# First weights issued beside x, later loads held back, and the first two chunks' roundings reordered in a four-layer kernel

## The reference, cut to what matters

```python
def _gemma_mlp(x, gate_w, up_w, down_w):          # 256 -> 1024 -> 256
    g = x @ gate_w; u = x @ up_w
    return (gelu(g) * u) @ down_w

# layer 0: softmax over 8 experts, the two best, their shares; plus one shared MLP
x = x + sum(w_e * _gemma_mlp(x, skill_e) for the two experts) + _gemma_mlp(x, shared)
# layer 1: the expert of the largest logit: silu(x @ W_up.T + b_up) * (x @ W_gate.T + b_gate), then @ W_down.T + b_down
# layer 2: x @ (sum_g y_g * weight_g * mask).T + bias
# layer 3: x @ W_base.T + b_base + 2 * sum_e w_e * (x @ A_e.T) @ B_e.T
```

## Time and profile before

| | us |
|---|---|
| median of three executions | 504.8 |
| span of the profiled execution, first to last instruction | 503.2 |
| PE busy in it | 495.4 |
| first product of layer 0 | 7.62 |
| PE idle before chunk 1 | 1.81 |
| ScalarE idle before it splits chunk 2 | 3.14 |

### The profile page before, as it was taken

One profiled execution on the slowest core, in us unless ns is written; L12 is line 12 of the kernel. 1 busy time (PEld: TensorE's weight loads), 2 busy tenths in 40 slices (PEclk: granted clock), 3 DMA queues, 4 the chain that ended last, 5 costly groups with the idle time before them and its releaser, 6 DMA issues.

```text
span 503.2 us, 7511 instructions
## 1 busy us (share of the span) xinstructions
PE 495.4 (98%) x2326; PEld 412.5 (82%) x2326; DVE 344.5 (68%) x566; ACT 250.9 (50%) x389; POOL 19.8 (4%) x36
## 2 busy tenths in 40 slices
PE   6999999999999999999999999999999999999997
PEld 5688688888888888888888888888888888888897
DVE  4657688985643767996653657888564376799666
ACT  4454444654554445564543644465454444556452
POOL 6003000000000020000000020000000002000000
PEclk9899999999999999999999999999999999999999
DMA  7848654139430233225732033213943023420001
GB/s 202 289 125 232 161 128 100 51 94 194 100 117 1 63 106 119 70 64 147 126 102 63 0 111 119 80 45 99 188 109 104 0 63 105 124 64 0 0 2 43
DMA packets 102995, 49.17 MB, mean 98 GB/s; under 512 B 53596, under 2 KB 101216, under 8 KB 102976
## 3 DMA queue, kind: packets, MB, share of 16 engines
q1 hardware_dynamic: 101200, 44.32, 32.8%
q0 software_dynamic: 1776, 4.62, 3.1%
HBM read 46.82 MB, written 2.10 MB: 97 GB/s over the span
## 4 chain that ended last, share of the span: by engine, by line
PE 96%; DMA 2%; SPq 1%; ACT 0%; issue 0%; DVE 0%; DVEq 0%
PE bank_a L940 10%; PE bank_a L941 10%; PE bank_a L942 10%; PE bank_b L942 10%; PE bank_b L941 10%; PE bank_b L940 10%; PE out L958 9%; PE out L962 9%; PE out L959 9%; DMA raw<-in_L_cond_shared_down 2%; PE tail L940 1%; PE tail L942 1%; PE tail L941 1%; PE tail L962 1%; PE tail L958 1%; PE tail L959 1%
## 5 line engine op out<-in xcount | busy, mean ns | idle before, releaser
L468 ACT ACTIVATE hid_hi<-hid 128x512 fp32r<-128x512 f32 x108 | 68.3, 632 | 105.2 <-DVE hid L587 63.0
L463 ACT ACTIVATE hid<-bank_a 128x512 f32<-128x512 f32 x96 | 57.3, 597 | 91.1 <-PE bank_a L942 91.1
L576 DVE TENSOR_TENSOR w_lo<-raw,w_hi 128x768 fp32r<-128x768 f32 x88 | 83.5, 949 | 3.3 <-ACT w_hi L455 3.3
L594 DVE TENSOR_TENSOR hid_lo<-hid,hid_hi 128x512 fp32r<-128x512 f32 x108 | 74.1, 686 | 14.0 <-ACT hid_hi L468 14.0
L587 DVE SCALAR_TENSOR_TENSOR hid<-bank_b,mine,hid 128x512 f32<-128x512 f32 x64 | 48.1, 751 | 46.7 <-PE bank_b L942 46.2
L455 ACT ACTIVATE w_hi<-raw 128x768 fp32r<-128x768 f32 x88 | 73.7, 838 | 3.1 <-DMA raw<-in_L_cond_shared_down 3.1
L940 PE MATMUL bank_a<-x_hi,w_hi 128*128 (+1 forms) x176 | 68.6, 390 | 0.0
L941 PE MATMUL bank_a<-x_lo,w_hi 128*128 (+1 forms) x176 | 68.6, 390 | 0.0
L942 PE MATMUL bank_a<-x_hi,w_lo 128*128 (+1 forms) x176 | 68.5, 389 | 0.0
L942 PE MATMUL bank_b<-x_hi,w_lo 128*128 (+1 forms) x176 | 68.5, 389 | 0.0
L940 PE MATMUL bank_b<-x_hi,w_hi 128*128 (+1 forms) x176 | 68.5, 389 | 0.0
(11 more groups left out here) (249 smaller groups left out, 711.0 us busy)
## 6 DMA issues: line engine op xcount, KB each, us to landing
raw<-in_L_cond_skill_gate SPq DMA_DIRECT2D x32, 256.0 KB, 2.9
raw<-in_L_cond_skill_up SPq DMA_DIRECT2D x32, 256.0 KB, 3.1
raw<-in_L_cond_skill_down SPq DMA_DIRECT2D x64, 128.0 KB, 3.2
raw<-in_L_cond_shared_down SPq DMA_DIRECT2D x26, 128.0 KB, 3.8
raw<-in_L_cond_shared_gate SPq DMA_DIRECT2D x12, 256.0 KB, 3.3
raw<-in_L_cond_shared_up SPq DMA_DIRECT2D x12, 256.0 KB, 3.5
early<-in_L_cond_weight POOLq DMA_DIRECT2D x2, 1024.0 KB, 8.9
raw_gate<-in_L_cond_W_gate SPq DMA_DIRECT2D x16, 128.0 KB, 3.1
```

The lines of the kernel that those rows point to most:

```text
L463: nc.scalar.activation(hid[:, n % 2], bank_a[n % 2][:, :], func, **kw).then_inc(act_ready, 1)
L468: nc.scalar.activation(hid_hi[:, n % 2], hid[:, n % 2], ACT.Copy).then_inc(hid_hi_ready, 1)
L576: nc.vector.tensor_tensor(lo, raw[:, raw_slot(i // 2), :, (i % 2) * P:(i % 2 + 1) * P], hi.bitcast(F32), ALU.subtract).then_inc(split_lo, 1)
L594: nc.vector.tensor_tensor(hid_lo[:, n % 2], hid[:, n % 2], hid_hi[:, n % 2].bitcast(F32), ALU.subtract).then_inc(hid_lo_ready, 1)
```

## The change

ScalarE's queue begins with the two loads of chunk 0's gate and up weights; SyncE issues them no more. GpSimd's loads from the base weights on wait until `split_lo` is 2, that is, until VectorE has done the down parts of chunks 0 and 1. VectorE itself makes the high part of chunk 0's gate and up weights and of both chunks' down weights (copies to fp32r), the latter in the new function `first_down_parts`: that of chunk 0 ahead of step 0, that of chunk 1 in step 0, behind `hidden`. ScalarE makes the high parts of x, then the routing's Exp, then the high part of chunk 1's gate and up, which has semaphores of its own (`second_hi`, `second_lo`), so that PE's chunk 1 waits for these alone. Two one-column activations (Exp, Gelu) are added ahead of the first uses of their functions. In step 0 of the first batch ScalarE makes `hidden_hi` before it splits chunk 2, and VectorE `hidden_lo` before its part of the split; the middle part of routing (`route_top2`) moves from the start of VectorE's list to step 0, behind that split.

```diff
--- before.py
+++ after.py
...
@@ -82,6 +57,10 @@
 
 def splits_done(b, i):
     return b * (CH - 2) + i + 1
+
+
+def highs_done(b, i):
+    return splits_done(b, i) - 2
 
 def tails_before(b):
     return b * 3 - 1 + len(PREPS) if not first(b) else len(PREPS)
@@ -213,7 +192,7 @@
         y_lora = sb("y_lora", [P, B])
         bias1_raw = sb("bias1_raw", [P, 2 * C1 + KD])
         bias1 = sb("bias1", [P, 2 * C1 + KD])
-        spare = sb("spare", [P, 1])
+        spare = sb("spare", [P, 3])
         mine = sb("mine", [P, PICK])
 
         bank_a = [ctx.enter_context(nc.psum_tensor(f"bank_a{n}", [P, S], F32)) for n in range(2)]
@@ -274,6 +253,9 @@
         x0_turned = sem("x0_turned")
         first_hi = sem("first_hi")
         first_lo = sem("first_lo")
+        second_hi = sem("second_hi")
+        second_lo = sem("second_lo")
+        first_down_hi = sem("first_down_hi")
         bank0_done = sem("bank0_done")
         end_hi = sem("end_hi")
         end_f = sem("end_f")
@@ -342,9 +324,10 @@
                 sp.dma_start(x_nat[:, 0, :, cols], x_rows[0][:, :, cols]).then_inc(x0_in[k], 16)
             for c in range(2):
                 cols = slice(c * P, (c + 1) * P)
-                for n, w in ((0, shared[0]), (2, shared[1])):
-                    sp.dma_start(raw[:, raw_slot(0), n:n + 2, cols],
-                                 w.rearrange("(k p) i -> p k i", p=P)[:, :, cols]).then_inc(first_in[c], 16)
+                if c == 1:
+                    for n, w in ((0, shared[0]), (2, shared[1])):
+                        sp.dma_start(raw[:, raw_slot(0), n:n + 2, cols],
+                                     w.rearrange("(k p) i -> p k i", p=P)[:, :, cols]).then_inc(first_in[c], 16)
                 sp.dma_start(raw[:, raw_slot(0), 4:6, cols], shared[2][cols, :].rearrange("p (j d) -> p j d", j=KD))\
                   .then_inc(first_down_in[c], 16)
             load_piece(1, None, *shared)
@@ -396,6 +379,7 @@
             nc.gpsimd.affine_select(out=expand[:, :], in_=expand[:, :], compare_op=ALU.is_ge, fill=0.0, base=R - 1,
                                     pattern=[[-1, P]], channel_multiplier=R).then_inc(const_pool, 1)
 
+            pool.wait_ge(split_lo, 2)
             pool.dma_start(base_nat, t["L3_cond_W_base"].rearrange("(k p) d -> p k d", p=P)).then_inc(turn_in, 16)
             for k in range(KD):
                 pool.dma_start(b3_nat[:, k], t["L3_cond_Bs"][:, k * P:(k + 1) * P, :].rearrange("e o r -> o e r"))\
@@ -440,18 +424,12 @@
         def _(act):
             def split(b, i):
                 p = i // 2
-                if i < 2:
-                    act.wait_ge(first_in[i], 32)
-                    act.wait_ge(first_down_in[i], 16)
-                else:
-                    act.wait_ge(raw_in[raw_slot(p)], 64 * raw_uses(b, p))
-                if i >= 2:
-
-                    if i - W_SLOTS >= 2:
-                        wait(act, down_done, hiddens_before(b) + hidden_of(b, i - W_SLOTS) + 1)
-                    elif not first(b):
-                        last = max(c for c in range(CH) if c >= 2 and (c - i) % W_SLOTS == 0)
-                        act.wait_ge(down_done, hiddens_before(b) - CH + last + 1)
+                act.wait_ge(raw_in[raw_slot(p)], 64 * raw_uses(b, p))
+                if i - W_SLOTS >= 2:
+                    wait(act, down_done, hiddens_before(b) + hidden_of(b, i - W_SLOTS) + 1)
+                elif not first(b):
+                    last = max(c for c in range(CH) if c >= 2 and (c - i) % W_SLOTS == 0)
+                    act.wait_ge(down_done, hiddens_before(b) - CH + last + 1)
                 nc.scalar.activation(split_slots(i)[0], raw[:, raw_slot(p), :, (i % 2) * P:(i % 2 + 1) * P],
                                      ACT.Copy).then_inc(split_hi, 1)
 
@@ -509,7 +487,7 @@
             def last_l1():
 
                 act.wait_ge(bias1_staged, B)
-                nc.scalar.activation(spare[:, :], bias1[:, 0:1], ACT.Silu)
+                nc.scalar.activation(spare[:, 0:1], bias1[:, 0:1], ACT.Silu)
                 for m in range(2 * C1):
                     slot = half_slot(m)
                     act.wait_ge(a_ready, hiddens_before(B) + m + 1)
@@ -526,9 +504,12 @@
                 for i in range(CH):
                     n = hidden_of(b, i)
                     activate(b, n, ACT.Gelu_apprx_tanh)
+                    if first(b) and i == 0:
+                        hidden_hi(b, n)
                     if i + SPLIT_AHEAD < CH:
                         split(b, i + SPLIT_AHEAD)
-                    hidden_hi(b, n)
+                    if not first(b) or i:
+                        hidden_hi(b, n)
                     if first(b) and i in PREP_AT:
                         prep_hi(PREP_AT[i])
                     if with_tail:
@@ -547,20 +528,20 @@
                     if turned(i - 1) is not None:
                         turn_chunk_hi(b, turned(i - 1))
 
+            for n, w in ((0, "gate"), (2, "up")):
+                act.dma_start(raw[:, raw_slot(0), n:n + 2, 0:P],
+                              t["L0_cond_shared_" + w].rearrange("(k p) i -> p k i", p=P)[:, :, 0:P]).then_inc(first_in[0], 16)
+            act.wait_ge(const_dve, 1)
+            nc.scalar.activation(spare[0:B, 1:2], ones[:, 0:1], ACT.Exp)
+            for k, ready in ((0, x0_turned), (1, tail_ready)):
+                act.wait_ge(ready, 1)
+                nc.scalar.activation(x_hi[:, k, 0:S], tail[:, k, :], ACT.Copy).then_inc(x_hi_ready, 1)
             act.wait_ge(route_step, 3)
             nc.scalar.activation(expo[:, :], logits[:, :], ACT.Exp, bias=neg_max[:, :],
                                  accum_out=zsum[:, :]).then_inc(exp_done, 1)
-            def first_x_hi(k, ready):
-                act.wait_ge(ready, 1)
-                nc.scalar.activation(x_hi[:, k, 0:S], tail[:, k, :], ACT.Copy).then_inc(x_hi_ready, 1)
-
-            act.wait_ge(first_in[0], 32)
-            nc.scalar.activation(res_hi[:, 0, 0:4], raw[:, raw_slot(0), 0:4, 0:P], ACT.Copy).then_inc(first_hi, 1)
-            first_x_hi(0, x0_turned)
-            first_x_hi(1, tail_ready)
-            act.wait_ge(first_down_in[0], 16)
-            nc.scalar.activation(res_hi[:, 0, 4:6], raw[:, raw_slot(0), 4:6, 0:P], ACT.Copy).then_inc(split_hi, 1)
-            split(0, 1)
+            act.wait_ge(first_in[1], 32)
+            nc.scalar.activation(res_hi[:, 1, 0:4], raw[:, raw_slot(0), 0:4, P:2 * P], ACT.Copy).then_inc(second_hi, 1)
+            nc.scalar.activation(spare[0:B, 2:3], ones[:, 0:1], ACT.Gelu_apprx_tanh)
             batch(0, False)
             with act.Fori(1, B) as b:
                 batch(b, True)
@@ -571,7 +552,7 @@
         @block.vector
         def _(dve):
             def split(b, i):
-                dve.wait_ge(split_hi, splits_done(b, i))
+                dve.wait_ge(split_hi, highs_done(b, i))
                 hi, lo = split_slots(i)
                 nc.vector.tensor_tensor(lo, raw[:, raw_slot(i // 2), :, (i % 2) * P:(i % 2 + 1) * P],
                                         hi.bitcast(F32), ALU.subtract).then_inc(split_lo, 1)
@@ -866,10 +847,15 @@
                         dve.wait_ge(mine_staged, b + 1)
                     m = i // MLP_CHUNKS
                     hidden(b, n, weight=mine[:, m - 1:m] if m else None)
+                    if first(b) and i == 0:
+                        first_down_parts(1)
+                        hidden_lo(b, n)
                     if i + SPLIT_AHEAD < CH:
                         split(b, i + SPLIT_AHEAD)
-                    hidden_lo(b, n)
+                    if not first(b) or i:
+                        hidden_lo(b, n)
                     if first(b) and i == 0:
+                        route_top2()
                         route_shares()
                     if first(b) and i in PREP_AT:
                         prep(PREP_AT[i])
@@ -906,20 +892,30 @@
             nc.vector.memset(warm, 0.0).then_inc(warm_ready, 1)
             nc.vector.memset(ones[:, :], 1.0).then_inc(const_dve, 1)
             route_maximum()
-            route_top2()
-            def first_x_lo(k):
+
+            def first_down_parts(c):
+
+                part = raw[:, raw_slot(0), 4:6, c * P:(c + 1) * P]
+                dve.wait_ge(first_down_in[c], 16)
+                nc.vector.tensor_copy(res_hi[:, c, 4:6], part).then_inc(first_down_hi, 1)
+                dve.wait_ge(first_down_hi, c + 1)
+                nc.vector.tensor_tensor(res_lo[:, c, 4:6], part, res_hi[:, c, 4:6].bitcast(F32), ALU.subtract)\
+                    .then_inc(split_lo, 1)
+
+            gate_up = [raw[:, raw_slot(0), 0:4, c * P:(c + 1) * P] for c in range(2)]
+            dve.wait_ge(first_in[0], 32)
+            nc.vector.tensor_copy(res_hi[:, 0, 0:4], gate_up[0]).then_inc(first_hi, 1)
+            dve.wait_ge(first_hi, 1)
+            nc.vector.tensor_tensor(res_lo[:, 0, 0:4], gate_up[0], res_hi[:, 0, 0:4].bitcast(F32), ALU.subtract)\
+                .then_inc(first_lo, 1)
+            for k in range(KD):
```

(23 more changed lines are left out.)

## The result

Median 500.78 us over four executions (499.39 to 501.62), beside 504.56 for the kernel before (503.96 to 505.85): ratio 0.9917, 95% interval 0.9893 to 0.994. Measured again over six executions: 499.38, ratio 0.9898, interval 0.9873 to 0.9923. The forecast was 500.6. The two profiled spans are further apart, 503.2 and 497.5: the changed kernel's trace belongs to its lowest execution, 499.39, and in every run here the time is 1.9 us above the span, so that the trace before stands for about 505.1, not for the median of 504.8.

The account below looks back on a forecast made before the run. Bound: the load of chunks 2 and 3, then VectorE's queue. Landing at 12.9 plus 5.8 puts chunk 1's down product at 18.7 instead of 22.86; 504.8 - 4.15 = 500.6 us, range 499.4 to 503.3.

Parts of the forecast that it names:

- piece 1's landing: Last load of shared-expert chunks 2 and 3: lands at 12.9 us instead of 16.42, bounds 11.7 and 15.25.
- rival 1: Load of chunks 2 and 3 lands at 12.2 or less, PE runs nearly through: gain 4.9, time 499.9; chance 0.13.
- down-product 1: PE's down product of chunk 1, behind the routing products: starts at 18.7 us instead of 22.86, gain 4.15.
- PE idleness: PE waits for chunk 2's low part from 14.4 to 14.8, then 0.7 us behind the routing products.
- first product: PE's start of chunk 0: at 7.4 us instead of 7.62, 0.2 won but not on the path.
- The chain behind it: Chunk 2's rounding, routing on VectorE, hidden 1 and its rounding: 5.8 us from landing to chunk 1's down product.
- Chunk 1: Waits for gate and up weights alone: they land at 8.0, low part at 9.4, no PE gap after chunk 0.
- Issuing from two queues: ScalarE issues the two first weight loads, so everything behind them on SyncE is issued 1.17 us sooner.
- Rival 2: Hardware queue gains only the issue time, load of chunks 2 and 3 lands at 15.25: 503.0 to 503.9; chance 0.13.
- The held loads: GpSimd's 0.88 MB for layers 2 and 3 wait until about 12.4; their effect on later x loads costed at nothing.
- Rival 3: Released GpSimd loads delay x of batch 1, PE stalls 6.4 us before its transposes: 507.0; chance 0.04.
- The slow clock: PE at 1.2 GHz from 14 to 15 us after 1.81 us idle before chunk 1: goes once that gap goes.

Follow-up runs that it names:

- r2: Changed kernel with the wait on GpSimd's queue removed, so its loads for layers 2 and 3 issue at once: 503.07 us, ratio 0.9974 to the kernel before.
- r4: Kernel before with only the wait on GpSimd's loads for layers 2 and 3 added: 500.91 us, ratio 0.9924.
- r5: Changed kernel with the old order of step 0, chunk 2 split before hidden 0's high and low parts: 499.85 us, ratio 0.9904 to the kernel before.
- r8: Changed kernel without any warm products on PE: 500.78 us, ratio 0.9918 to the kernel before.
- r3: Changed kernel with chunk 0's gate and up loads issued by SyncE behind x again, none by ScalarE: 499.81 us, ratio 0.9902 to the kernel before.
- r6: Kernel before with only the new order of step 0, hidden 0 before the split of chunk 2: 503.86 us, ratio 0.9982.
- r12: Changed kernel with one more warm product at the start and one between the transposes of x's halves: 500.14 us, ratio 0.9899 to the kernel before.
- r1: Changed kernel measured again without an edit: 499.38 us, ratio 0.9898 to the kernel before.
- r10: Changed kernel with GpSimd's base weights load issued ahead of the wait, the rest held: 501.53 us, ratio 0.9922 to the kernel before.
- r11: Changed kernel with GpSimd's two Bs loads issued ahead of the wait, the rest held: 501.13 us, ratio 0.9917 to the kernel before.

## Why the prediction was right

The direction and the place are right: piece 1's landing was the bound, and taking GpSimd's loads off the engines moved it (r2, r4). The case that happened is rival 1, to which I gave 0.13: PE runs through. That 500.6 fits the first median of 500.78 to 0.2 us is luck. Three of those four executions lie in the upper group; the lower one, 499.39, and the second median, 499.38, are 1.2 us below the forecast and at the very edge of its range, 499.4. In the traces down-product 1 comes at 17.23 and not at 18.7: 1.1 us of PE idleness that I forecast (0.4 before chunk 2, 0.7 before down-product 1) is not there, and the first product is 0.5 us earlier.

- **The landing of piece 1, the mis-sized term.** Forecast 12.9, measured 11.1 (r5, same loads) and not waited for in the changed kernel. I had let the hardware queue need the same 9.5 us of engine time as before and taken the 74.1% from 2 to 6 us as given. In r5 the two hardware queues had 74.1 + 22.4% there, 0.9 us of engine time more, and 90.6% from 6 to 11.1, some 8.5 us in all until the landing: 1.0 less than I let them need, with 2.40 MB moved where the kernel before had moved 2.67 by its landing. The earlier issue, which I left out, was there as well: 6.65 against 7.74 before.
- **The chain behind it.** Landing plus 5.8 was right where it binds: 5.5 in r2. In the changed kernel it ends at 16.93, before PE wants it, so the 0.7 us of idleness that I forecast did not come.
- **The first product.** 6.93 instead of 7.4. Second half of x at 6.02 (forecast 5.8); but its four transposes took 0.66 and not 1.1. The 1.1 is the figure of the trace before, and r8, without warm products, has 1.11 again. With PE alone on the path these 0.5 us count, which I had written off as not on it.
- **Chunk 1.** Low part done at 8.87 (forecast 9.4), no gap. Copies on VectorE 0.43 and 0.28 us, inside the bounds.
- **Issuing from two queues.** Worth 0.4 us in r3. Rival 2 failed, since the landing was not bound by the issue: the share of the engines that was set free was the matter (r2, r4). The rule of the Trainium skill on issuing engines ("DMA: Bandwidth & Descriptors", section "SWDGE vs HWDGE vs iDMA") says that only the issue time is saved; r3 agrees with its 0.4 us, less than the 1.17 of issue time that moved.
- **The held loads.** They fell on nothing: PE never waited for x of batch 1. Rival 3 did not come.
- **The slow clock.** I wrote that its cause goes with the gap. Not shown: r6 has 2.06 us of idleness and no fall, r12 a fall without idleness. And the fall in the trace before (8 matmuls 0.2 us longer, 13.5 to 16.9) was not worth anything on the path. PE came out of it and still waited, for the rounding behind piece 1's landing:

```profile
16.46 0.59 PE L942 MATMUL bank_b<-x_hi,res_lo 128*128 128x512 f32 x1
17.86 0.50 PE L958 MATMUL out<-hid_hi,res_hi 128*128 128x512 f32 x1 [0.80 <-ACT hid_hi L468]
```

The executions agree: the kernel before beside r1 has 503.92 and 504.13 with a mean clock of 0.997, and 503.88 and 504.49 with 1.000. (It also has 506.28 with 0.997; a fall at another place, as in r12, would do that, but no trace shows it.) So the 5.64 us between the two traces hold no price of a fall. The change is worth 4.75 us by the lowest times in the same batch (503.88 and 499.13), 5.2 by the medians there, and 3.8 by the first medians, three quarters of whose executions after the change lie in the upper group.

## What to carry to other kernels

When the first work waits for a load, look at what else is on the DMA engines in that time before anything else: loads not wanted for 20 us, held back by one wait, gave seven tenths of this gain. Add up the queue of the engine behind a landing, since it says how much of an earlier landing counts and at which point the next bound takes over. And when the granted clock of a trace falls, look at what its engine does next: a slow stretch ahead of a wait costs nothing, one in a stream without waits costs half its length. A slow start shows in the spacing of the first matmuls and not in the granted clock.

## What the runs showed of the hardware

- A load of 128 KB lands 8.6 us after its issue with GpSimd's loads beside it and 4.5 without (r2, r5).
- TensorE's granted clock fell to 0.50 for 3.4 us while PE was busy in every window (r12, also r10), and stayed at 1.00 behind 2.06 us of idleness (r6).
- Matmuls of 512 columns stood 0.43 us apart at the start while the granted clock read 1.00 (r2, r8, r11).
- The table load of 1.28 us ended at 9.45 in the changed kernel and the next activation began at 9.46. There it lies ahead of the first gelu at 9.57; what the one-column gelu has to do with it no run shows, as none leaves it out.
